# Products into an unread bank in the pauses of TensorE around the scan and in the feed stage

## The chip, the cores and the metric

The kernel runs on one core of one Trainium2 chip (trn2). The metric is the device time of the launch in microseconds (us), lower is better; the figure of a kernel is the median of its runs. One profiled execution gives the trace. In it the clock granted to TensorE is shown as a share of 2.4 GHz: 1.00 is the upper of its two levels, 0.50 is 1.2 GHz.

## What is computed

A decoder of two layers in float32 over x of shape (4, 256, 128), with 16 heads of 8 features. Each of the six blocks reads a layer norm of x and adds its result to x:

```
x = x + L0_attn(layernorm(x))               # cumulative linear attention
x = x + L0_xattn(layernorm(x), ctx)         # cross attention, masked by length
x = x + L0_ffn(layernorm(x))                # two rounds of top-2 of 8 experts
x = x + L1_attn(layernorm(x))               # state space scan, 16 states
x = x + L1_xattn(layernorm(x), ctx)         # cross attention with a bias and a padding mask
x = x + L1_ffn(layernorm(x))                # feed stage: two quantised linear layers
```

The three blocks that matter here:

```
# L1_attn: proj = x @ W_xproj; delta = softplus(proj[:64] @ W_dt + b_dt)
# dA = exp(clip(delta*A)); R = exp(cumsum(log dA)); S = cumsum(delta*B*x / R)
# y = sum over 16 states of C * (R*S)  + x*D
# L1_xattn: softmax(q.k/sqrt(8) + bias, padded keys out) @ v, then @ Wo + bo
def bitlinear(x, w, b):                     # L1_ffn: gelu between two of them
    xq = act_quant(rmsnorm(x))              # rounded to 8 bits with a scale for each row
    return einsum('bsd,fd->bsf', xq, weight_quant(w)) + b
```

## The kernel before

The 1024 tokens lie as 8 tiles (j) of 128 rows; much of the work goes by half, 4 tiles or 512 tokens at a time. There is one program for each engine, written out in order by hand; nothing is scheduled by a planner. An engine runs its program strictly in order and waits where the program has a wait on a semaphore (`wait_ge`), so on TensorE (PE) each product starts only when all that stand before it have been issued. PSUM has eight banks of 128 x 512 float32; `bank(i)` is one of them, and every use of each bank is fixed in the code.

The program of TensorE is the function `_(pe)` at L2108. It calls in turn `self_tensor`, `cross_tensor(pe, 0)`, `experts_tensor`, `half_turn(pe, 1, 5)`, `scan_tensor`, `cross_tensor(pe, 1)` and `feed_tensor`. Three places in it matter.

**Entry of the scan.** `half_turn` (L1365) transposes the second half of the normalised rows XN into bank 5 once VectorE (DVE) has normalised them (L1358). ScalarE (ACT) copies that to XNT (L1370). `scan_tensor` then forms the 64 step inputs (`scan_steps_in`, L1471, into bank 0), the rows of B and C (`scan_rows_in`, L1479, bank 4) and delta (`scan_delta_in`, L1487, bank 1). ACT and DVE make the softplus of it (L1498, L1535) and split the B and C rows (L1526 to L1529). After that comes the loop over 16 states: DVE runs for each state a scan with a floor (`carry`, L1705), a product (`accumulate`, L1711) and a second scan (`advance`, L1718). TensorE spreads rows of B and C over the partitions in it (`row`, L287) and sums the outputs (`gather`, L1571). The result is transposed (L1594) and added to X (L1748).

**Entry of the second cross attention.** In `cross_tensor(pe, 1)` stand in order: `entry_turn` (L266), the transposes of the first normalised half; `first_queries((0, 1))` (L697), the queries of batch 0 for two groups of heads; the first scores (L711, 16 records: 4 heads); `first_queries((2, 3))`; `queries(1)` (L687); then the loop, which begins with scores of two more heads. ACT copies a group of queries to QP (L916) before its scores can run. DVE takes maxima of the scores with the bias added (L988) and, after the first four heads, normalises the second half (L252 to L257), which the next `entry_turn` waits for.

**Feed stage.** The first half of the hidden products runs in the shadow of the cross attention (`feed_turn(pe, 0)`, `feed_first(pe, 0)` to `3`). `feed_tensor` holds the rest: `feed_turn` (L1898) transposes quantised rows of the second half, `feed_first(j)` (L1905) is the first layer for tile j, `turn_hidden(j)` (L1915) transposes the quantised hidden rows of tile j, ACT copies them (L1971), and `second(j)` (L1924) is the second layer. DVE computes the quantisation (L1846, L1849), the hidden rows (L1821), their peaks (L1827), the factors (L1779 to L1790) and adds the result to X (`finish`, L1856). GpSimd (POOL) takes powers for the factors (L1987).

`identb` is the 128 x 128 identity in bfloat16 and `wq1` the quantised weights of the first feed layer, 128 x 512 in bfloat16; both are ready well before the scan.

Of the kernel before, what the change touches and what calls it, by code (L numbers as in the profile page):

```python
# [53 lines left out]
def build(nc, inp, out):  # L54
    ctx = ExitStack()
    with ctx:
        def sb(name, shape, dt=F32):
            return ctx.enter_context(nc.sbuf_tensor(name, shape, dt))
# [3 lines left out]
        def sig(name):  # L62
            if name not in signals:
                signals[name] = ctx.enter_context(nc.semaphore(name))
            return signals[name]
# [21 lines left out]
        identb = sb("identb", [P, P], BF16)  # L87
# [82 lines left out]
        wq1 = sb("wq1", [P, FF], BF16)  # L170
# [12 lines left out]
        def bank(i):  # L183
            return PS[:, i, :]

        def halfbank(i):
            return bank(i).bitcast(BF16)
# [73 lines left out]
        def entry_turn(pe, e, half):  # L261
            pe.wait_ge(sig("xn"), 2 * ENTRY_XN[e] + half + 1)
            if e and half == 1:
                pe.wait_ge(sig("queries"), (e - 1) * B + 2)
            for t in range(4):
                ins = pe.transpose(bank(ENTRY_BANK[e][half])[:, t * P:(t + 1) * P], XN[:, 4 * half + t, :], ident[:, :])  # L266
            ins.then_inc(sig("turned"), 1)
# [6 lines left out]
        def key_bias(dve):  # L274

            dve.wait_ge(sig("const_late"), 1)
            dve.wait_ge(sig("bqk_in"), 16 * HG)
            dve.wait_ge(sig("row_bias"), 1)
            for w, scale in ((0, DH ** -0.5), (1, 1.0)):
                a = rowbias[:, 1, w, :]  # L280
                ins = dve.scalar_tensor_tensor(a, bqk[:, :, w], scale, a, ALU.mult, ALU.add)
            ins.then_inc(sig("bias_rows"), 1)

        def project(pe, first_bank, lhsT, rhs, signal):

            for half in range(2):
                ins = pe.matmul(bank(first_bank + half)[0:lhsT.shape[1], :], lhsT,  # L287
                                rhs[:, half * HALF:(half + 1) * HALF], start=True, stop=True)
            ins.then_inc(sig(signal), 1)
# [377 lines left out]
        def first_query(g):  # L667

            return bank(6 + g % 2)[:, (g // 2) * S:(g // 2 + 1) * S]

        def cross_tensor(pe, L):
# [19 lines left out]
            def first_queries(gs):  # L691

                pe.wait_ge(sig("xnt"), 2 * 5 + 1)
                for g in gs:
                    if g >= 2:
                        pe.wait_ge(sig("query_taken"), g - 1)
                    pe.matmul(first_query(g), WP[:, 1, g, :], XNT[:, 0:S], start=True, stop=True)\  # L697
                        .then_inc(sig("query_part"), 1)
# [98 lines left out]
                ins.then_inc(sig("proj_out"), 1)  # L797

            pe.wait_ge(sig("wp"), 2)
            entry_turn(pe, L + 1, 0)  # L800
            if L == 0:
                queries(0)
            else:
                first_queries((0, 1))
            pe.wait_ge(sig("neg_rows"), 16 * HG * (L + 1))
            pe.wait_ge(sig("key_rows"), 16 * H * (L + 1))
# [301 lines left out]
        def pass_logits(pe, p):  # L1108
            pe.wait_ge(sig("xnt"), 4 + p + 1)
            for t in range(4):  # L1110
                ins = pe.matmul(bank(LOGITS_BANK[p])[:, t * NE:(t + 1) * NE], XNT[:, tokens_of(p)][:, t * P:(t + 1) * P],
                                router[:, :], start=True, stop=True)
            ins.then_inc(sig("logits"), 1)
# [49 lines left out]
        def experts_tensor(pe):  # L1163

            def down(m):

                pe.wait_ge(sig("gated"), 2 * m + 2)
                if m:
                    pe.wait_ge(sig("mixed"), m)
                for t in range(4):  # L1170
                    for c in range(2):
                        ins = pe.matmul(bank(6)[:, t * P:(t + 1) * P], E6[:, (2 * m + c) % 4, t * P:(t + 1) * P],  # L1172
                                        W2[:, m % NE, c, :], start=(c == 0), stop=(c == 1))
                ins.then_inc(sig("down"), 1)

            for g in range(3, UNITS_MOE):
                p, n = divmod(g, UPS)
                unit_up(pe, g)
                if g % 2 == 1:
                    down((g - 3) // 2)  # L1180
                if p + 1 < PASSES and n == 6:
                    pass_turn(pe, p + 1)
                if p + 1 < PASSES and n == 8:
                    pass_logits(pe, p + 1)
                if p == 0 and n in HALVES:
                    context_half_tensor(pe, HALVES.index(n))
                if p == 1 and n in HALVES:
                    keys_half_tensor(pe, HALVES.index(n))
                if p == 1 and n == 14:
                    pe.wait_ge(sig("keys"), 2)  # L1190
                    pe.wait_ge(sig("w_sums"), 1)
                    pe.matmul(bank(7)[:, 0:2], onesf, wscale[:, :], start=True, stop=True).then_inc(sig("w_total"), 1)
                if p == 3 and n == 10:
                    pe.wait_ge(sig("logits_read"), 4)
                    half_turn(pe, 0, 7)
                if p == 3 and n == 12:
                    scan_steps_in(pe, 0, SCAN_BANK[0][0])
                if p == 3 and n == 13:
                    scan_rows_in(pe, 0, SCAN_BANK[0][1])
                if p == 3 and n == 15:  # L1200
                    scan_delta_in(pe, 0, SCAN_BANK[0][2])
            down(UNITS_MOE // 2 - 1)
# [159 lines left out]
        def half_turn(pe, half, bk):  # L1362
            pe.wait_ge(sig("xn"), 2 * 4 + half + 1)
            for t in range(4):
                ins = pe.transpose(bank(bk)[:, t * P:(t + 1) * P], XN[:, 4 * half + t, :], ident[:, :])  # L1365
            ins.then_inc(sig("turned"), 1)
# [527 lines left out]
        def feed_turn(pe, half):  # L1894
            pe.wait_ge(sig("q1"), half + 1)
            for t in range(4):
                j = 4 * half + t
                ins = pe.transpose(halfbank(0)[:, t * P:(t + 1) * P], QB[:, j * P:(j + 1) * P], identb[:, :])  # L1898
            ins.then_inc(sig("q_turned"), 1)

        def feed_first(pe, j):
            pe.wait_ge(sig("qt1"), j // 4 + 1)
            if j >= 2:
                pe.wait_ge(sig("h1_read"), j - 1)
            pe.matmul(bank(1 + j % 2), QTB[:, j * P:(j + 1) * P], wq1[:, :], start=True, stop=True)\  # L1905
                .then_inc(sig("h1"), 1)

        def feed_tensor(pe):

            def turn_hidden(j):  # L1910
                pe.wait_ge(sig("q2"), j + 1)
                if j >= 2:
                    pe.wait_ge(sig("gt"), j - 1)
                for c in range(FF // P):
                    ins = pe.transpose(halfbank(3 + j % 2)[:, c * P:(c + 1) * P], GQ[:, j % 2, c * P:(c + 1) * P],  # L1915
                                       identb[:, :])
                ins.then_inc(sig("g_turned"), 1)

            def second(j):
                pe.wait_ge(sig("gt"), j + 1)  # L1920
                if j >= 2:
                    pe.wait_ge(sig("x_tile"), j - 1)
                for c in range(FF // P):
                    ins = pe.matmul(bank(6 + j % 2)[:, 0:D], GQT[:, j % 2, c * P:(c + 1) * P], wq2[:, c, :],  # L1924
                                    start=(c == 0), stop=(c == FF // P - 1))
                ins.then_inc(sig("h2"), 1)

            feed_turn(pe, 1)
            feed_first(pe, 4)
            feed_first(pe, 5)  # L1930
            turn_hidden(0)
            feed_first(pe, 6)
            second(0)
            turn_hidden(1)
            feed_first(pe, 7)
            second(1)
            turn_hidden(2)
            second(2)
            turn_hidden(3)
            second(3)  # L1940
            turn_hidden(4)
            for j in range(5, NT):
                turn_hidden(j)
                second(j - 1)
            second(NT - 1)

        def feed_root(act, ch):
# [160 lines left out]
        @block.tensor  # L2108
        def _(pe):
            pe.wait_ge(sig("ident"), 1)  # L2110
            entry_turn(pe, 0, 0)
            entry_turn(pe, 0, 1)
            self_tensor(pe)
            cross_tensor(pe, 0)
            experts_tensor(pe)
            half_turn(pe, 1, 5)
            scan_tensor(pe)
            cross_tensor(pe, 1)
            feed_tensor(pe)
# [101 lines left out]
```

## Time and profile before

| | us |
|---|---|
| runs shown | 612.29, 613.69, 617.9 |
| median | 613.69 |
| profiled execution, its device time | 612.31 |
| profiled execution, span from first to last instruction | 610.5 |
| mean granted clock of TensorE in it | 0.913 |

Busy in the span: TensorE 503.1 us (82%), its weight loads 288.7 us, VectorE 451.9 us (74%), ScalarE 263.1 us, GpSimd 134.5 us. The profile has a row for each engine over 40 equal slices of 15.3 us, and one with the granted clock. The chain that ended last follows the end of the program back through whatever released each step. A product in float32 shows in the trace as two records, and each record is preceded by a load of its weights.

### The profile page before, as it was taken

How to read it: one execution, taken by the hardware profiler on the slowest of the kernel's cores; microseconds unless marked ns; L12 is line 12 of the kernel's file. 1: busy time of each engine (PE TensorE's matmuls, PEld its weight loads, DVE VectorE, ACT ScalarE, POOL GpSimd, SP SyncE). 2: the span in 40 equal slices, each digit the busy share in tenths (PEclk: the TensorE clock that was granted, in tenths of full speed). 3: DMA queues.
4: the chain of work that ended last, by engine and by line, in shares of the span. 5: the costliest groups of instructions: out<-in, count | busy, mean ns of one | idle time of the engine just before them, and what ended most of it. 6: DMA issues, size and time to landing. Idle time of an engine off the chain costs nothing.

```text
span 610.5 us, 8920 instructions
## 1 busy us (share of the span) xinstructions
PE 503.1 (82%) x3146; PEld 288.7 (47%) x3146; DVE 451.9 (74%) x1175; ACT 263.1 (43%) x455; POOL 134.5 (22%) x101
## 2 busy tenths in 40 slices
PE   3997799999999999999999545475475999999433
PEld 1344666665666666666665301122123655555212
DVE  6499767776673567666475779999995688888785
ACT  5531356555543244244242345555511444445552
POOL 8443000000000000310000028999980100000100
PEclk9999899999999999999999755978886999999855
DMA  5000160000100000100000000000001000000001
GB/s 131 24 15 1 34 209 2 1 2 2 43 2 0 1 1 5 31 6 0 1 1 1 1 0 0 0 0 1 0 1 43 2 1 2 2 2 1 2 4 30
DMA packets 10767, 9.25 MB, mean 15 GB/s; under 512 B 2050, under 2 KB 9540, under 8 KB 10724
## 3 DMA queue, kind: packets, MB, share of 16 engines
q1 hardware_dynamic: 10724, 8.69, 5.2%
q8 instruction: 25, 0.41, 0.3%
q14 instruction: 18, 0.15, 0.1%
HBM read 6.98 MB, written 0.52 MB: 12 GB/s over the span
## 4 chain that ended last, share of the span: by engine, by line
PE 63%; DVE 29%; ACT 3%; issue 3%; POOL 0%; DVEq 0%; POOLq 0%; ACTq 0%
PE PS L1146 18%; PE PS L711 10%; PE PS L1172 9%; DVE PS L1705 6%; DVE VA L1718 6%; PE PS L774 5%; DVE PS L1711 3%; PE PS L759 3%; PE PS L750 3%; PE PS L687 2%; PE PS L731 2%; PE PS L450 1%; PE PS L428 1%; PE PS L784 1%; DVE E L557 1%
## 5 line engine op out<-in xcount | busy, mean ns | idle before, releaser
L1146 PE MATMUL PS<-XNT,KSA 128*128 128x512 f32 x256 | 118.3, 596 | 0.0
L933 ACT ACTIVATE E<-PS 128x512 f32<-128x512 f32 x128 | 71.2, 596 | 67.2 <-PE PS L759 41.7
L1160 DVE TENSOR_TENSOR E<-E,PS 128x512 f32<-128x512 f32 x64 | 43.9, 687 | 55.3 <-ACT E L1154 54.4
L1154 ACT ACTIVATE E<-PS 128x512 f32<-128x512 f32 x64 | 38.1, 597 | 105.3 <-PE PS L1146 105.0
L759 PE MATMUL PS<-QM,KP 32*128 32x256 f32 x512 | 81.3, 399 | 0.8 <-ACT E L933 0.8
L711 PE MATMUL PS<-KP,QP 32*128 32x256 f32 x512 | 78.2, 409 | 0.8 <-ACT QP L900 0.8
L1172 PEld LDWEIGHTS PS<-KSA,E 128*128 128x128 f32 x512 | 62.1, 192 | 16.0 <-issue 14.7
L1146 PEld LDWEIGHTS PS<-XNT,KSA 128*128 128x128 f32 x256 | 45.2, 191 | 41.5 <-issue 41.3
L1172 PE MATMUL PS<-KSA,E 128*128 128x128 f32 x512 | 62.4, 275 | 0.4 <-DVE XN L1381 0.4
L711 PEld LDWEIGHTS PS<-KP,QP 32*128 32x128 f32 x512 | 51.1, 188 | 20.9 <-issue 10.3
L988 DVE CUSTOM_DVE_ANT_0 SCR<-PS,KSA 128x256 f32<-128x256 f32 x128 | 46.5, 420 | 19.5 <-PE PS L711 18.4
L287 PE MATMUL PS<-KSA,select 128*128 128x512 bf16 x64 | 25.8, 495 | 41.7 <-ACT KSA L1606 31.9
L759 PEld LDWEIGHTS PS<-QM,KP 32*128 32x128 f32 x512 | 53.6, 184 | 3.7 <-issue 3.3
L983 DVE TENSOR_REDUCE MXT<-PS 128x2 f32<-128x512 f32 x64 | 41.1, 686 | 18.1 <-PE PS L711 18.0
L2094 POOL TENSOR_SCALAR KSA<-SCR 128x512 f32<-128x512 f32 x1 | 0.6, 618 | 199.5 <-DVE wq L1775 199.5
L1381 DVE SCALAR_TENSOR_TENSOR XN<-PS,gates,XN 128x128 f32<-128x128 f32 x124 | 34.8, 344 | 7.8 <-PE PS L1172 7.8
L1652 POOL TENSOR_SCALAR OT<-OT 128x1020 f32<-128x1020 f32 x16 | 16.6, 1036 | 101.3 <-ACT OT L1625 100.2
L1571 PE MATMUL PS<-E,ident 128*128 128x512 f32 x60 | 35.6, 726 | 3.2 <-POOL E L1667 3.2
L1705 DVE TENSOR_TENSOR_SCAN PS<-OT,PS 128x1024 f32<-128x1024 f32 x16 | 36.7, 2294 | 0.5
L287 PEld LDWEIGHTS PS<-KSA,select 128*128 128x128 bf16 x64 | 5.2, 108 | 66.3 <-ACT KSA L1606 42.1
L1667 POOL TENSOR_TENSOR E<-VA 128x1024 f32<-128x1024 f32 x15 | 35.2, 2349 | 3.8 <-PE PS L1571 2.9
L1659 POOL TENSOR_TENSOR KSA<-SCR,KSA 128x1024 f32<-128x1024 f32 x15 | 35.2, 2349 | 0.9 <-ACT KSA L1606 0.9
(278 smaller groups left out, 827.8 us busy)
## 6 DMA issues: line engine op xcount, KB each, us to landing
KSA<-in_w SPq DMA_DIRECT2D x2, 1024.0 KB, 6.8
X<-in_x SPq DMA_DIRECT2D x2, 256.0 KB, 3.2
SCR<-in_ctxT SPq DMA_DIRECT2D x1, 512.0 KB, 5.4
KP<-OT SPq DMA_DIRECT2D x16, 32.0 KB
SCR<-in_fside SPq DMA_DIRECT2D x1, 512.0 KB, 4.8
KP<-QM SPq DMA_DIRECT2D x16, 32.0 KB
out_x<-X SPq DMA_DIRECT2D x8, 64.0 KB, 1.5
wx<-in_w_x SPq DMA_DIRECT2D x1, 384.0 KB, 6.5
```

Source lines behind the costliest of these rows:

```text
L711: ins = pe.matmul(score_bank(n, i)[:, q * S:(q + 1) * S], QP[rows(i), g, t:t + P], KP[rows(i), g, b * S:(b + 1) * S], start=True, stop=Tru ...
L759: ins = pe.matmul(o[:, kt * S:(kt + 1) * S], KP[rows(i), g, t:t + P], QM[rows(i), g, b * S:(b + 1) * S], start=not parts_of_bias(j), stop= ...
L933: act.activation(slot(m, j), weight_bank(m, j), ACT.Exp).then_inc(sig("exps"), 1)
L983: ins = dve.tensor_reduce(MXT[:, n % 2, :, c], o, AX, ALU.max, negate=True)
L988: ins = dve.tensor_tensor_reduce(out=BIASED[:, i % 2, q, :], in0=o[:, q, :], in1=BIASQ[:, q, :], scale=-1.0, scalar=3e38, op0=ALU.add, op1 ...
L1146: ins = pe.matmul(bank(2 * (g % 3) + o), w[:, e, c * P:(c + 1) * P], XNT[:, tokens_of(p)], start=True, stop=True)
L1154: act.activation(E6[:, 4 + g % 2, :], bank(2 * (g % 3)), ACT.Silu).then_inc(sig("silu"), 1)
L1160: dve.tensor_tensor(E6[:, g % 4, :], E6[:, 4 + g % 2, :], bank(2 * (g % 3) + 1), ALU.mult)\
L1172: ins = pe.matmul(bank(6)[:, t * P:(t + 1) * P], E6[:, (2 * m + c) % 4, t * P:(t + 1) * P], W2[:, m % NE, c, :], start=(c == 0), stop=(c = ...
L1571: ins = pe.matmul(bank(6 + half), ident[:, :], HC[n % 2][:, half * HALF:(half + 1) * HALF], start=(n == 0), stop=False, skip_group_check=True)
L1705: dve.tensor_tensor_scan(CARRY, DA[n % 3], FLOOR, 0.0, ALU.mult, ALU.add).then_inc(sig("carried"), 1)
L1718: dve.tensor_tensor_scan(HH[n % 2], DA[n % 3], CARRY, 0.0, ALU.mult, ALU.add).then_inc(sig("state"), 1)
```

## The change

A new helper `turn_over(pe, bk, n)` issues n products of `identb` with `wq1` (128x128 by 128x512, bfloat16) into a bank bk. No instruction reads what they write, they carry no semaphore, and they wait for none. 124 of them are put into TensorE's program: 20 ahead of the transposes at the entry of the scan and 2 behind (bank 1), 16 and 2 around the transposes at the entry of the second cross attention (bank 2), and 84 in 16 places of the feed stage (bank 5). Nothing is removed, and the programs of the other engines are the same.

```diff
--- before.py
+++ after.py
@@ -281,6 +281,11 @@
                 ins = dve.scalar_tensor_tensor(a, bqk[:, :, w], scale, a, ALU.mult, ALU.add)
             ins.then_inc(sig("bias_rows"), 1)
 
+        def turn_over(pe, bk, n):
+
+            for _ in range(n):
+                pe.matmul(bank(bk), identb[:, :], wq1[:, :], start=True, stop=True)
+
         def project(pe, first_bank, lhsT, rhs, signal):
 
             for half in range(2):
@@ -797,10 +802,13 @@
                 ins.then_inc(sig("proj_out"), 1)
 
             pe.wait_ge(sig("wp"), 2)
+            if L == 1:
+                turn_over(pe, 2, 16)
             entry_turn(pe, L + 1, 0)
             if L == 0:
                 queries(0)
             else:
+                turn_over(pe, 2, 2)
                 first_queries((0, 1))
             pe.wait_ge(sig("neg_rows"), 16 * HG * (L + 1))
             pe.wait_ge(sig("key_rows"), 16 * H * (L + 1))
@@ -1925,23 +1933,36 @@
                                     start=(c == 0), stop=(c == FF // P - 1))
                 ins.then_inc(sig("h2"), 1)
 
+            turn_over(pe, 5, 28)
             feed_turn(pe, 1)
+            turn_over(pe, 5, 2)
             feed_first(pe, 4)
             feed_first(pe, 5)
+            turn_over(pe, 5, 16)
             turn_hidden(0)
             feed_first(pe, 6)
+            turn_over(pe, 5, 1)
             second(0)
+            turn_over(pe, 5, 2)
             turn_hidden(1)
             feed_first(pe, 7)
+            turn_over(pe, 5, 1)
             second(1)
+            turn_over(pe, 5, 2)
             turn_hidden(2)
+            turn_over(pe, 5, 2)
             second(2)
+            turn_over(pe, 5, 2)
             turn_hidden(3)
+            turn_over(pe, 5, 2)
             second(3)
+            turn_over(pe, 5, 12)
             turn_hidden(4)
             for j in range(5, NT):
+                turn_over(pe, 5, 2)
                 turn_hidden(j)
                 second(j - 1)
+                turn_over(pe, 5, 2)
             second(NT - 1)
 
         def feed_root(act, ch):
@@ -2113,7 +2134,9 @@
             self_tensor(pe)
             cross_tensor(pe, 0)
             experts_tensor(pe)
+            turn_over(pe, 1, 20)
             half_turn(pe, 1, 5)
+            turn_over(pe, 1, 2)
             scan_tensor(pe)
             cross_tensor(pe, 1)
             feed_tensor(pe)
```

TensorE's program at the entry of the scan, before: the last product of the experts (L1172, into which the transposes L1365 follow), up to the spread rows L287.

```order
L1172 MATMUL PS<-KSA,E 128x128 x8
L1365 MATMUL PS<-ident,XN 128x128 x4
L1471 MATMUL PS<-XNT,wssm 64x512
L1479 MATMUL PS<-XNT,wssm 32x512 x4
L1487 MATMUL PS<-SCR,wdt 128x512
L287 MATMUL PS<-KSA,select 128x512 x18
```

The same place in the changed kernel, where lines are numbered 5 to 8 higher and L287 is the new helper (the name `wq` stands for `wq1`).

```order
L1180 MATMUL PS<-KSA,E 128x128 x8
L287 MATMUL PS<-wq,identb 128x512 x20
L1373 MATMUL PS<-ident,XN 128x128 x4
L287 MATMUL PS<-wq,identb 128x512 x2
L1479 MATMUL PS<-XNT,wssm 64x512
L1487 MATMUL PS<-XNT,wssm 32x512 x4
L1495 MATMUL PS<-SCR,wdt 128x512
```

Only the two new rows have come in; the order of the rest is as it was. At the entry of the second cross attention TensorE's program reads, in the changed kernel:

```order
L1602 MATMUL PS<-ident,SCR 128x128 x8
L287 MATMUL PS<-wq,identb 128x512 x16
L266 MATMUL PS<-ident,XN 128x128 x4
L287 MATMUL PS<-wq,identb 128x512 x2
L702 MATMUL PS<-XNT,WP 128x256 x2
L716 MATMUL PS<-KP,QP 128x256 x8
L702 MATMUL PS<-XNT,WP 128x256 x2
L692 MATMUL PS<-XNT,WP 128x256 x4
```

Here too the two rows of L287 are all that is new: one behind the transposes of the scan's result, one behind the transposes of the normalised half. In the feed stage, from the last `feed_first` in the cross attention's shadow on, the changed kernel has:

```order
L1913 MATMUL PS<-wq,SCR 128x512
L287 MATMUL PS<-wq,identb 128x512 x28
L1906 MATMUL PS<-identb,SCR 128x128 x4
L287 MATMUL PS<-wq,identb 128x512 x2
L1913 MATMUL PS<-wq,SCR 128x512 x2
L287 MATMUL PS<-wq,identb 128x512 x16
L1923 MATMUL PS<-identb,SCR 128x128 x4
L1913 MATMUL PS<-wq,SCR 128x512
L287 MATMUL PS<-wq,identb 128x512
L1932 MATMUL PS<-wq,SCR 128x128 x4
L287 MATMUL PS<-wq,identb 128x512 x2
```

L1906, L1913, L1923 and L1932 are the L1898, L1905, L1915 and L1924 of before. Every wait of TensorE in this stage now has one or more products of the helper ahead of it.

## Rows read from the trace of the kernel before

**Rows 1.** Page: granted clock, in tenths, in 40 slices of 15.3 us.

```profile
PEclk9999899999999999999999755978886999999855
```

**Rows 2.** Windows: us, busy us of PE, PEld, DVE, ACT, POOL (records), granted clock, DMA.

```profile
343.50:346.30 2.80, 0.00 (x0) 0.00 (x0) 2.04 (x11) 0.41 (x2) 0.00 (x0) 0.50 0.00 0
380.00:455.00 75.00, 45.56 (x104) 16.69 (x103) 73.69 (x40) 36.23 (x46) 69.56 (x36) 0.86 0.00 0
465.40:473.20 7.80, 7.05 (x29) 4.71 (x30) 1.87 (x11) 2.32 (x6) 0.00 (x0) 0.50 0.14 46
```

**Rows 3.** Timeline of PE at the scan's entry: start, us, line, form [idle before].

```profile
346.34 1.12 PE L1365 MATMUL PS<-ident,XN 128*128 128x128 f32 x4 [5.30 <-DVE XN L1358]
348.24 1.94 PE L1471 MATMUL PS<-XNT,wssm 128*64 128x512 f32 x2 [0.78 <-ACT XNT L1370]
350.11 1.94 PE L1479 MATMUL PS<-XNT,wssm 128*32 128x512 f32 x8
351.97 2.07 PE L1487 MATMUL PS<-SCR,wdt 64*128 64x512 f32 x2
```

**Rows 4.** Timeline of PE: the same kinds at the full clock.

```profile
326.41 1.07 PE L1471 MATMUL PS<-XNT,wssm 128*64 128x512 f32 x2
...
331.11 1.06 PE L1479 MATMUL PS<-XNT,wssm 128*32 128x512 f32 x8
...
337.52 1.12 PE L1487 MATMUL PS<-SCR,wdt 64*128 64x512 f32 x2
...
477.51 0.66 PE L266 MATMUL PS<-ident,XN 128*128 128x128 f32 x4
```

**Rows 5.** Chain that ended last: start us, us, what; three products like the helper's.

```profile
480.85 0.65 PE PS L750 x3
```

**Rows 6.** Timeline of PE, second cross attention's entry; last row of the first's.

```profile
465.39 1.09 PE L266 MATMUL PS<-ident,XN 128*128 128x128 f32 x4 [5.49 <-DVE XN L257]
467.22 2.08 PE L697 MATMUL PS<-XNT,WP 128*128 128x256 f32 x4 [0.74 <-ACT XNT L271]
469.22 2.11 PE L711 MATMUL PS<-KP,QP 32*128 32x256 f32 x16
471.27 2.08 PE L697 MATMUL PS<-XNT,WP 128*128 128x256 f32 x4
473.13 1.94 PE L687 MATMUL PS<-XNT,WP 128*128 128x256 f32 x8
...
68.75 1.17 PE L711 MATMUL PS<-KP,QP 32*128 32x256 f32 x16 [0.77 <-ACT QP L900]
```

**Rows 7.** Timeline of PE in the scan: pauses, and the products behind them.

```profile
407.41 0.60 PE L287 MATMUL PS<-KSA,select 128*128 128x512 bf16 x2 [2.67 <-ACT KSA L1606]
407.85 3.10 PE L1571 MATMUL PS<-E,ident 128*128 128x512 f32 x4
...
425.16 0.61 PE L287 MATMUL PS<-KSA,select 128*128 128x512 bf16 x2 [1.80 <-ACT KSA L1606]
425.60 1.88 PE L1571 MATMUL PS<-E,ident 128*128 128x512 f32 x4
...
454.04 1.99 PE L1571 MATMUL PS<-E,ident 128*128 128x512 f32 x4 [2.62 <-POOL E L1667]
```

**Rows 8.** Timeline of PE in the feed stage; the first row at the full clock.

```profile
567.29 0.39 PE L1898 MATMUL PS<-identb,SCR 128*128 128x128 bf16 x4
...
582.14 0.61 PE L1898 MATMUL PS<-identb,SCR 128*128 128x128 bf16 x4 [7.29 <-DVE SCR L1816]
...
597.09 0.61 PE L1924 MATMUL PS<-wq,SCR 128*128 128x128 bf16 x4 [0.69 <-ACT SCR L1971]
600.74 0.61 PE L1915 MATMUL PS<-identb,SCR 128*128 128x128 bf16 x4 [3.04 <-DVE SCR L1849]
603.94 0.61 PE L1915 MATMUL PS<-identb,SCR 128*128 128x128 bf16 x4 [1.30 <-DVE SCR L1849]
```

**Rows 9.** Timeline of POOL: the power that the second factors wait for.

```profile
596.75 1.01 POOL L1987 TENSOR_TENSOR rs<-ve,exponent 128x4 f32<-128x4 f32 x1 [10.79 <-DVE ve L1835]
```

## The prediction

> **What bounds the kernel now.** I read the page's row of the granted clock first: TensorE runs at its upper level for most of the span and falls from it in the slices around the scan and in the last two and a half [rows 1]. The rest asks, for each of those stretches, whether a slow TensorE is on the path that sets the end. I read that from the chain of waits, then from the timeline of PE.
>
> In the loop of the scan it is not. From 380 to 455 us VectorE is busy 73.69 of 75 us while the clock is only 0.86 on average [rows 2]; the chain goes round in VectorE's three instructions and passes TensorE nowhere. A faster TensorE buys nothing there, and the change puts nothing there.
>
> It is on the path at three places, each behind a pause:
> - Entry of the scan. PE pauses 5.30 us for the last normalised half [rows 3]. The clock is at 0.50 from 343.5 us on [rows 2], so the transposes, step inputs, B and C rows and delta all run at 1.2 GHz, end to end, and ACT and DVE wait behind them.
> - Entry of the second cross attention. PE pauses 5.49 us [rows 6]; from 465.4 to 473.2 us it is busy 7.05 of 7.8 us at 0.50 [rows 2].
> - Feed stage. The first pause is 7.29 us [rows 8], and the clock stays low to the end [rows 1]. DVE sets most of this stage; TensorE is only in some links of it.
>
> **Entry of the scan, term A.** The change fills the pause with 20 products. The nearest row is L750, the same shape (128x128 identity, 512 columns, bfloat16): three take 0.65 us on the chain at full clock, 0.217 each [rows 5]. 20 take 4.33 us of the 5.30, so 0.97 us is left idle and the transposes aren't held up. The two products behind them (0.43 us) lie in the 0.78 us in which PE waits for ACT's copy [rows 3]. If the clock stays up, each row at the slow clock is exchanged for the same kind at the full one [rows 3, 4]: transposes 1.12 to 0.66 (0.46), step inputs 1.94 to 1.07 (0.87), B and C rows 1.94 to 1.06 (0.88), delta 2.07 to 1.12 (0.95). A = 3.2 us. They lie on the chain one behind the other. What is late next is DVE's and ACT's own work on delta, which moves along with them. After it PE goes idle and the clock may fall again; the spread rows (L287) are then slow as before, and the loop doesn't care.
>
> **Entry of the second cross attention, term B.** 16 products take 3.47 us of 5.49, which leaves a pause of 2.02 us; then transposes, and two products (0.43 us) in a gap of 0.74 us [rows 6]. At full clock: transposes 1.09 to 0.66 (0.43) [rows 4, 6]; first scores 2.11 to 1.17, by the same 16 records of the first cross attention (0.94) [rows 6]; each pair of queries (L697) has no row at full clock, so I scale L687, the same shape, eight in 1.94 us of which half is 0.97 to 1.1 with its tail: 2.08 to 1.08, twice (2.0) [rows 6]. Sum 3.37. ACT's copy of the first queries would then be ready just behind the second pair of them, not ahead, which I put at 0.1 us. B = 3.3 us. DVE starts its maxima earlier by the same amount, and its normalisation of the second half, which the next transposes wait for, still ends before PE arrives there, so the gain isn't given back. The bias that DVE adds later is loaded long before.
>
> Does the clock stay up through a pause of 2.02 us? The scan shows both outcomes. Behind a pause of 1.80 us four products took 1.88 us, all at full clock; behind one of 2.62 us they took 1.99; but behind one of 2.67 us they took 3.10, so the clock was lost in between [rows 7]. A pause of 2.02 lies among these, and what follows it is thin: transposes, 0.43 us of products and a small gap. I hold B for a little more likely kept than lost. In A (0.97 us left) and in the feed stage below I hold it for likely.
>
> **Feed stage, term C.** 28 products take 6.08 us of the 7.29, 12 take 2.6 of the 3.04, and the four between later tiles 0.87 of 1.30 [rows 8]; the groups of one and two lie under ACT's copies (0.69 us idle before L1924 [rows 8]). Four bfloat16 transposes take 0.61 us slow and 0.39 fast [rows 8], so each such group on the chain is worth 0.22. Where transposes and second layer run back to back at the end of a round, both count, 0.44. On the chain: the transposes at 582.14 (0.22); nothing from then to 595 us, where the chain runs through ACT and DVE and leaves PE out; nothing in the round of tile 3 either, though the chain shows PE there: the products end at 597.70, but POOL's power for the next factors ends at 597.76 [rows 8, 9], so it takes PE's place; then the rounds of tiles 5, 6 and 7 (0.44 each). C = 1.5 us.
>
> **Cost.** No engine but PE gets an instruction, no queue is passed and no wait is added, so what a product can hold up is only what stands behind it in PE's order. At full clock all of it fits, cost 0. At the slow clock one takes about 0.43 (twice 0.217), and the fit is gone: see the second and last rival.
>
> **Sum.** Against the profiled execution's own 612.31 us: 612.31 - 3.2 - 3.3 - 1.5 = 604.3. The median of the runs stands 1.4 us above that execution. I take this as scatter that the change leaves alone: where the clock happens to be low at the end of the scan, a set of output sums there takes 3.10 instead of 1.88 us [rows 7], and those are on the chain. So 605.7 against the median of 613.69.
>
> **A rule beside it.** At full clock four float32 transposes take 0.66 us and at the slow clock 1.09 [rows 4, 6]; so they follow the clock, and A and B count them. The Trainium skill ("TensorE: Matmul & The Clock Gate", Part 4, PE-mode transpose) says that the full clock does not engage for transposes, which don't count as busy in the same way. On the duration the trace disagrees (by that half of the rule A, B and C would shrink by 0.46, 0.43 and four times 0.22, and the time be 607.5; it gets no chance). On the other half no row here decides. If they don't count, the stretch behind the remaining 2.02 us pause looks emptier still; that is my second case below with a mechanism, at 609.1, and I leave its chance as that case has it.
>
> **The rivals.**
> 1. All three kept: 605.7. Chance 0.45.
> 2. The clock falls in the 2.02 us pause all the same. B is lost, and the two products behind the transposes run slow, 0.87 us in a 0.74 us gap, 0.1 late: 612.31 - 4.7 + 0.1 = 607.7, with the 1.4 us 609.1. For it: the 2.67 us pause. Against: 2.62 us survived. In part (the clock back sooner than before) it ends between. Chance 0.32.
> 3. The feed stage falls too, since every tile's round holds short pauses: C gone, A and B kept, 612.31 - 6.5 = 605.8, or 607.2. Chance 0.1.
> 4. The products don't hold the clock anywhere but cost nothing: within 1 us of 613.7. Against: L750, the same product among others, runs at the full clock [rows 5]. Chance 0.08.
> 5. Slower. The products run at 1.2 GHz: 20 take 8.7 us against 5.30 (3.4 late), 28 take 12.2 against 7.29 (4.9 late), 12 take 5.2 against 3.04 (2.2 late), the four 1.7 against 1.30 (0.4, three times), 16 take 6.9 against 5.49 (1.5): 13 us, 627. It decides only if the clock falls before the products start. A filler run may have 0.97 / 0.217, about 4, slow ones of 20 before it delays anything. The run follows on dense work at full clock in all three places, so I give 0.05.
>
> **How the numbers follow.** The forecast is that of case 1, 605.7. The range goes down to no scatter and a B fuller by the 0.1 and by more in executions that stayed slow for longer: 603.3; and up past case 2 with its scatter: 610.0. About 1%, 6.1 us, is what a measurement of this kernel can tell from no change: the border is 607.55. Case 1 gives 0.38 below it, case 3 0.07, case 2 0.08: faster 0.53. Slower by over 1% only in case 5: 0.04. The rest, 0.43, within 1%.
>
> **What would show it.** In the profile after: the granted clock at 1.00 from the last expert product to delta, with L1471, L1479 and L1487 (now L1479, L1487, L1495) near 1.07 us each; the scan's first step 3.2 us earlier from the last expert product; the loop still 5.9 us for each state. For B, the clock row between the last transposes of the scan and the first scores, and those at 1.17 us. For C, groups of four transposes at 0.39 us to the end, and the round of tile 3 no shorter. I am wrong if the clock is up and a place isn't shorter (then something else stood right behind TensorE, most likely in C, where POOL and DVE are close), or if rows of the helper are what L1373, L266 or L1923 wait for.

## The result

The changed kernel takes 609.35 us, the median of 15 runs (607.46 to 611.78); the kernel before takes 613.69 us over 15 runs beside them (611.14 to 618.17). The ratio is 0.9937, with a 95% interval of 0.9914 to 0.9960: about 4 us less, half of the 8.0 us forecast. The time lies within the forecast range, but the size of the gain was wrong, and its main term, B, is where it failed.

A count given ahead of the prediction is too high: the diff adds up to 122 products and not 124, with 82 in 17 places of the feed stage and not 84 in 16. The traces agree: the trace of the changed kernel has 122 loads of the products' weights, that of the kernel with the feed stage's products alone has 82. No price in the prediction hangs on it.

The profiled execution took 611.73 us, span 610.0, mean granted clock 0.944 (0.913 before). Its row of the granted clock, in 40 slices, answers to [rows 1]:

```profile
PEclk9999799999998899999999985987788999999899
```

The low slices at the end are gone, and those around the scan are fewer. But there are new low tenths in the middle, where the program is as before: in the experts the clock fell twice, for 3.4 us each. The timeline of PE there (start, us, line, form) shows what one such fall costs:

```profile
184.86 1.88 PE L1154 MATMUL PS<-XNT,KSA 128*128 128x512 f32 x4
...
189.91 3.53 PE L1154 MATMUL PS<-XNT,KSA 128*128 128x512 f32 x4
```

The same four records take 1.88 us at full clock and 3.53 behind the fall, 1.65 more. With a third fall at 152 us and a longer one at 63 us, the last expert product ends at 346.81 us here and at 341.05 in the profile of before. So the two profiled executions differ by only 0.5 us in their spans, though the three places that the change touches are 6.3 us shorter. At the entry of the scan, the timeline of PE, to be read against [rows 3]:

```profile
344.79 2.02 PE L1180 MATMUL PS<-KSA,E 128*128 128x128 f32 x16 [0.38 <-DVE XN L1389]
346.87 4.26 PE L287 MATMUL PS<-wq,identb 128*128 128x512 bf16 x19
352.12 0.66 PE L1373 MATMUL PS<-ident,XN 128*128 128x128 f32 x4 [0.99 <-DVE XN L1366]
352.62 0.59 PE L287 MATMUL PS<-wq,identb 128*128 128x512 bf16 x2
353.56 1.04 PE L1479 MATMUL PS<-XNT,wssm 128*64 128x512 f32 x2 [0.35 <-ACT XNT L1378]
354.53 1.06 PE L1487 MATMUL PS<-XNT,wssm 128*32 128x512 f32 x8
355.53 1.12 PE L1495 MATMUL PS<-SCR,wdt 64*128 64x512 f32 x2
```

(One record of the 20 is missing from the trace.) 0.99 us of the pause is left, 0.97 was forecast; each of the four groups has the full clock's duration, and the loop starts 17.27 us after the last expert product instead of 20.42. At the entry of the second cross attention, to be read against [rows 6]:

```profile
462.56 3.40 PE L287 MATMUL PS<-wq,identb 128*128 128x512 bf16 x15
467.90 0.66 PE L266 MATMUL PS<-ident,XN 128*128 128x128 f32 x4 [1.94 <-DVE XN L257]
468.40 0.59 PE L287 MATMUL PS<-wq,identb 128*128 128x512 bf16 x2
469.31 1.88 PE L702 MATMUL PS<-XNT,WP 128*128 128x256 f32 x4 [0.32 <-ACT XNT L271]
471.12 2.04 PE L716 MATMUL PS<-KP,QP 32*128 32x256 f32 x16
473.08 1.13 PE L702 MATMUL PS<-XNT,WP 128*128 128x256 f32 x4
```

Behind the 1.94 us that are left of the pause the clock is lost all the same, but later than the forecast's second case has it. The transposes and the two products behind them are still fast (granted clock 1.00 from 467.90 to 469.30 us); then most of the first queries and the first scores are slow (0.50 from 469.60 to 472.90 us), and the second queries are fast again. In the feed stage, to be read against [rows 8]:

```profile
575.33 0.60 PE L1913 MATMUL PS<-wq,SCR 128*128 128x512 bf16 x1
575.72 7.72 PE L287 MATMUL PS<-wq,identb 128*128 128x512 bf16 x28
583.28 0.39 PE L1906 MATMUL PS<-identb,SCR 128*128 128x128 bf16 x4
...
606.16 0.40 PE L1923 MATMUL PS<-identb,SCR 128*128 128x128 bf16 x4 [0.44 <-DVE SCR L1857]
606.39 0.39 PE L1932 MATMUL PS<-wq,SCR 128*128 128x128 bf16 x4
```

The clock had fallen at 575.4 us, so the 28 products took 7.72 us instead of the 6.1 counted, and no idle time stands before L1906: the transposes were held up by 0.3 us. To the end of the program every group of four then takes 0.39 or 0.40 us.

### The profile page after: what moved, and what is told of

Its sections match the earlier page's. It is cut to its first block, busy times and chain, and to the rows that moved or that the text cites. A ratio compares the mean times of both kernels' runs of the same rounds, so it can differ in the third digit from the quotient of the medians.

```text
span 610.0 us, 9155 instructions
## 1 busy us (share of the span) xinstructions
PE 526.7 (86%) x3260; PEld 298.6 (49%) x3268; DVE 452.4 (74%) x1175; ACT 263.2 (43%) x455; POOL 134.5 (22%) x101
## 4 chain that ended last, share of the span: by engine, by line
PE 66%; DVE 23%; issue 5%; ACT 4%; POOL 2%; POOLq 0%; DVEq 0%; ACTq 0%
PE PS L1154 18%; PE PS L716 10%; PE PS L1180 9%; PE PS L779 5%; DVE PS L1713 5%; DVE VA L1726 5%; PE PS L764 3%; PE PS L755 3%; DVE PS L1719 2%; PE PS L692 2%; PE PS L736 2%; PE PS L455 1%; PE PS L287 1%; PE PS L433 1%; PE PS L789 1%
## 5 line engine op out<-in xcount | busy, mean ns | idle before, releaser
L1154 PE MATMUL PS<-XNT,KSA 128*128 128x512 f32 x256 | 121.5, 609 | 0.0
L779 PE MATMUL PS<-E,VX 128*32 128x256 f32 x512 | 35.2, 393 | 0.7 <-ACT E L941 0.7
```

Of the source, the lines that this page charges most:

```text
L779: ins = pe.matmul(bank(6)[rows(i), (g % 2) * S:(g % 2) * S + S], VX[:, QT * b + kt, HG * g + i, :], slot(m, j)[:, kt * S:(kt + 1) * S], st ...
L1154: ins = pe.matmul(bank(2 * (g % 3) + o), w[:, e, c * P:(c + 1) * P], XNT[:, tokens_of(p)], start=True, stop=True)
```

## Experiments

The theories, as the expectations number them. **Theory 1:** what the change is worth at its three places can be read in each trace, B is worth less than forecast because the clock falls in the 2 us left of its pause, and what else moves comes from falls of the clock elsewhere, the same in both kernels. **Theory 2:** the new products delay the dense part ahead of them. **Theory 3:** a clock kept at one place falls at the next, so the gain is given back. **Theory 4:** the falls in the experts come from one-row products there. A fall is a stretch in which the granted clock is at the lower level.

All are edits of the changed kernel unless said otherwise. Since one trace shows one execution, I read each trace by stretches: to the last expert product; from there to the first scan instruction of DVE; from there to the end of the transposed result (the loop); from there to the first L750 product (the entry of the second cross attention); and the feed stage from the transposes in the cross attention's shadow to the end. (Where an expectation gives the entry of the second cross attention as 20.95 and 19.2 us, it is the stretch that has 20.79 and 19.03 us here.) The cross attention between the last two takes 86.60 to 86.62 us in all the traces in which both of its ends could be read.

| trace | products | to experts' end | scan entry | loop | cross entry | feed |
|---|---|---|---|---|---|---|
| before | none | 341.05 | 20.42 | 98.43 | 20.79 | 43.25 |
| none | none | 342.70 | 20.43 | 98.43 | 20.76 | 43.24 |
| none2 | none | 341.71 | 19.51 | 98.44 | 20.39 | 43.24 |
| scan_entry | 22 | 340.73 | 17.26 | 98.44 | 20.65 | 43.27 |
| cross_entry | 18 | 342.42 | 19.48 | 99.56 | 17.71 | 43.26 |
| feed | 82 | 342.75 | 20.43 | 98.43 | 20.79 | 41.57 |
| after | 122 | 346.81 | 17.27 | 98.44 | 19.03 | 41.85 |
| again | 122 | 338.50 | 17.26 | 99.67 | 18.94 | 41.85 |
| look1 | 122 | 344.15 | 17.26 | 99.67 | 18.93 | 41.87 |
| look2 | 122 | 341.20 | 17.26 | 98.43 | 20.41 | 41.58 |
| look3 | 122 | 339.15 | 17.27 | 99.60 | 19.03 | 41.84 |
| pause24 | 130 | 341.08 | 17.26 | 98.44 | 17.71 | 41.56 |
| rows128 | none | 335.89 | 19.20 | 99.77 | 19.58 | 43.44 |
| all | 127 and 4 others | 336.90 | 17.26 | 99.26 | 17.71 | 41.57 |

**None of the products**, as a control: every call of the helper replaced by `pass`.

> None of the 124 products, the rest of the changed kernel as it is: the kernel before in other words. Every theory: ratio 1.000 within its interval. What it is for is its trace, a second execution of the kernel before. Theory 1 (the clock also falls at random in the dense parts ahead of the scan, the same in both kernels): the last expert product ends somewhere between 341 and 347 us, not at one place, and the granted clock shows short stretches at 0.50 ahead of 340 us wherever it ends late. Theory 2 (the products delay the dense part of the changed kernel): it ends at 341 us as in the profile of the kernel before, with no stretch at 0.50 between 70 and 340 us.

614.05 us against 613.04 of before, ratio 1.0034 (1.0011 to 1.0057). (The ratio is not simply that of the two medians, which is 1.0016.) The two have the same instructions, and still the interval leaves out 1. So a ratio here can be off by another 0.3%, about 2 us, beyond its interval, and verdicts on single terms of 1 or 2 us have to come from the stretches of the traces. The trace fits theory 1: its experts end at 342.70 us, with one fall of the clock in them.

**Only the scan's entry:** the two calls at the second cross attention and all 13 of the feed stage are replaced.

```diff
-                turn_over(pe, 2, 16)
+                pass
...
-                turn_over(pe, 2, 2)
+                pass
...
-            turn_over(pe, 5, 28)
+            pass
...
```

> Only the 22 products at the entry of the scan. From the end of the last expert product to the first scan instruction of DVE: 17.3 us against 20.4, as in the changed kernel. Theory 1: ratio 0.9950 (3.1 us off), all of it kept to the end. Theory 3 (a gain at one place is lost at the next pause, since the clock falls there all the same): less than half of it is left at the end, ratio above 0.997.

610.06 us, ratio 0.9944 (0.9923 to 0.9965), the largest of the three single parts, with 17.26 us at the scan's entry and the stretches behind it as before. The ratio is that of 3.4 us, and the trace shows none of the 3.2 us lost at the next pause (20.65 us there, 20.79 before); theory 3 falls.

**Only the second cross attention's entry:** the calls of the feed stage and these are replaced.

```diff
-            turn_over(pe, 1, 20)
+            pass
             half_turn(pe, 1, 5)
-            turn_over(pe, 1, 2)
+            pass
```

> Only the 18 products at the entry of the second cross attention. From the end of the transposes of the scan's result to the first group of L750: 20.95 us before, 19.2 in the profile of the changed kernel, where the clock fell for 3.4 us. Theory 1 (a pause of 2 us is left, in which the clock falls in most executions): 19 to 20.9 us, ratio 0.997. Forecast's theory (the clock is kept): 17.6 us, ratio 0.9946.

612.58 us, ratio 0.9988 (0.9959 to 1.0016). In its trace the clock held, and the entry took 17.71 us, 3.1 less: the rows of PE show what B is worth when it is kept.

```profile
466.84 0.65 PE L266 MATMUL PS<-ident,XN 128*128 128x128 f32 x4 [1.94 <-DVE XN L257]
467.34 0.59 PE L287 MATMUL PS<-wq,identb 128*128 128x512 bf16 x2
468.25 1.13 PE L702 MATMUL PS<-XNT,WP 128*128 128x256 f32 x4 [0.32 <-ACT XNT L271]
469.60 1.17 PE L716 MATMUL PS<-KP,QP 32*128 32x256 f32 x16 [0.23 <-ACT QP L924]
```

The runs together show less: 0.5 us by the medians against the kernel before, and 1.5 against the kernel without the products, which ran beside them. In how many of them the clock held can't be read from the times. The 1.94 us of pause that are left are the same here as in the changed kernel, so that pause can be survived.

**Only the feed stage:** the calls at both entries are replaced.

```diff
-            turn_over(pe, 1, 20)
+            pass
...
-                turn_over(pe, 2, 16)
+                pass
...
```

> Only the 84 products of the feed stage. Forecast's theory: 1.5 us, ratio 0.9975. Rival: the first run of 28 holds up the transposes behind it (by 0.3 us in the profile of the changed kernel, where it took 7.7 us instead of 6.1 because the clock was at 0.50 for 3.4 us), so 1.2 us or less, ratio 0.998 or above.

611.85 us, ratio 0.9992 (0.9971 to 1.0013), which by itself tells nothing from no change. Its trace has 41.57 us against 43.25 in the feed stage, 1.7 less, with no fall of the clock there.

**The changed kernel again**, and three more single executions of it:

> The changed kernel a second time, for a second trace of it and to see by how much a repeated comparison moves. Theory 1 (what the change is worth at its three places is fixed within 1.5 us; the rest of the difference between two executions comes from falls of the clock ahead of the scan): from the last expert product to the scan loop 17.3 us again; entry of the second cross attention 17.7 (clock kept) or 19 to 21 us (fallen); feed stage 41.5 to 41.9; the experts 185.8 us or 1.65 us more for each fall of the clock in them. Ratio 0.990 to 0.994. Theory 2 (the products delay the dense part): the first cross attention and the experts together again 288 us against 282.4.

607.99 us, ratio 0.9911 (0.9875 to 0.9946). In this trace the experts take 185.84 us, as before, and the first cross attention 97.4 us against 96.6: together 283 us, not the 288 of theory 2. So the products do not slow the dense part ahead of them; theory 2 falls. The cross entry took 18.94 us.

> The changed kernel once more, for its trace alone. What is open is how often the clock survives the 2 us that are left of the pause at the entry of the second cross attention: it fell in both traces so far (19.0 and 18.9 us) and held in the one with the products only there (17.7). Theory 1: 17.7 when it holds, 18.9 to 21 when it falls, nothing between; more falls than holds. The forecast's chance (held in 4 or 5 of 10) would want 17.7 in one or two of three looks. Scan entry 17.3 and cross attention 86.6 in each.

> As the look before: 17.7 us or 18.9 to 21 us at the entry of the second cross attention, 17.3 at the scan's entry, 41.5 to 41.9 in the feed stage; the experts 185.8 us plus 1.65 for each fall of the clock in them.

> As the two looks before. If all three traces show 17.7 us, the size of B was right and what was missing of the gain lies in the scatter alone; if none does, B is worth about 1.8 us with 16 products.

One execution each: 610.19, 607.21 and 605.21 us. The cross entry took 18.93, 20.41 and 19.03 us. With the two earlier traces that makes none kept in five; with the trace of `cross_entry`, which has the same products at this place, one in six. In look2 the fall lasted longer, and even the projections behind the scores are slow:

```profile
462.28 0.66 PE L266 MATMUL PS<-ident,XN 128*128 128x128 f32 x4 [1.94 <-DVE XN L257]
462.78 0.68 PE L287 MATMUL PS<-wq,identb 128*128 128x512 bf16 x2
463.69 2.08 PE L702 MATMUL PS<-XNT,WP 128*128 128x256 f32 x4 [0.23 <-ACT XNT L271]
465.69 2.11 PE L716 MATMUL PS<-KP,QP 32*128 32x256 f32 x16
467.73 2.08 PE L702 MATMUL PS<-XNT,WP 128*128 128x256 f32 x4
469.60 2.08 PE L692 MATMUL PS<-XNT,WP 128*128 128x256 f32 x8
```

The scan's entry is 17.26 or 17.27 us in all of them, as expected. In look2 the clock was up at the start of the feed stage as well, and the run of 28 took what was counted for it, with the transposes waiting for DVE and not for the run:

```profile
571.29 6.21 PE L287 MATMUL PS<-wq,identb 128*128 128x512 bf16 x28
578.76 0.40 PE L1906 MATMUL PS<-identb,SCR 128*128 128x128 bf16 x4 [1.26 <-DVE SCR L1824]
```

look3 shows the loop's weak place, the last sums of the outputs, here behind a fall of the clock; the same four records take 1.99 us in the row of before at 454.04 us [rows 7]:

```profile
449.12 3.68 PE L1579 MATMUL PS<-E,ident 128*128 128x512 f32 x4 [2.63 <-POOL E L1675]
```

**The kernel without the products again:**

> The kernel without the products once more, for a third trace of it: 20.4 us at the scan's entry, 20.8 at the second cross attention's, 43.2 in the feed stage. Theory 1: these three do not move, so that the gain per place does not depend on the execution of before; the rest of its span (self attention, first cross attention, experts, end of the scan) moves by 1 to 6 us.

One execution, 611.66 us. The scan's entry took 19.51 us and not 20.4: the clock fell as before but came back sooner, so that delta, the last of the four groups, was fast (1.16 us; the other three slow, 1.11, 1.94 and 1.93):

```profile
347.01 1.11 PE L1373 MATMUL PS<-ident,XN 128*128 128x128 f32 x4 [5.30 <-DVE XN L1366]
348.90 1.94 PE L1479 MATMUL PS<-XNT,wssm 128*64 128x512 f32 x2 [0.78 <-ACT XNT L1378]
350.77 1.93 PE L1487 MATMUL PS<-XNT,wssm 128*32 128x512 f32 x8
352.64 1.16 PE L1495 MATMUL PS<-SCR,wdt 64*128 64x512 f32 x2
```

So my expectation was wrong that the stretches of before are the same in every execution; what the products save is 3.15 us in one and 2.25 in another.

**24 products instead of 16** at the second cross attention's entry:

```diff
-                turn_over(pe, 2, 16)
+                turn_over(pe, 2, 24)
```

> The changed kernel with 24 products instead of 16 ahead of the transposes at the entry of the second cross attention: 5.2 us of the pause of 5.5, so about 0.3 us of it is left instead of 2. Theory 1 (what loses B is the clock falling in the 2 us that are left): entry 17.7 us with no stretch at 0.50 in it, ratio below that of the changed kernel by 0.002. Rival (other things set that entry): 19 us or more all the same. If the clock is low when the run begins, the products are slow and the transposes come late by up to 1.5 us.

605.28 us, ratio 0.9874 (0.9848 to 0.9899), beside 0.9911 for the changed kernel in the same comparison: 2.7 us less by the medians, though the intervals overlap. Its trace:

```profile
462.17 0.66 PE L266 MATMUL PS<-ident,XN 128*128 128x128 f32 x4 [0.22 <-DVE XN L257]
462.66 0.59 PE L287 MATMUL PS<-wq,identb 128*128 128x512 bf16 x2
463.57 1.13 PE L702 MATMUL PS<-XNT,WP 128*128 128x256 f32 x4 [0.31 <-ACT XNT L271]
464.93 1.17 PE L716 MATMUL PS<-KP,QP 32*128 32x256 f32 x16 [0.22 <-ACT QP L924]
```

0.22 us of the pause is left instead of 1.94, every group is fast, and the entry takes 17.71 us. The rival, that something else sets that entry, falls: it has the 17.71 us of `cross_entry`, where the clock held. That the fuller pause is what holds the clock rests on few traces (held in two of two with 24 products, this one and `all`, and in one of six with 16) and on the ratio, which points the same way.

**Full rows for the bias products** of the experts stage, on the kernel without the helper's products:

```diff
-        brow = sb("brow", [1, D])
+        brow = sb("brow", [P, D])
...
-                ins = pe.matmul(o, onesf[0:1, :], brow[0:1, :], start=False, stop=True)
+                ins = pe.matmul(o, onesf, brow[:, :], start=False, stop=True)
...
+            pool.memset(brow[:, :], 0.0)
```

> The kernel before, but the products that add the value bias of the second cross attention in the experts (eight float32 products, one row deep: a row of ones with the bias row) are made 128 rows deep, of a full matrix of ones and a bias tile that is zero below its first row: the same sum, in the same number and size of records. Theory 4 (the falls of the clock near 186 to 200 us come from these thin products): no fall between 180 and 205 us, experts 185.8 us. Rival (the falls there are at random or belong to the whole stretch of short products): falls in 2 of 3 executions as before, 187.5 or 189.2 us in this profile. Ratio 0.998 by theory 4, 1.000 by the rival.

609.41 us, ratio 0.9931 (0.9899 to 0.9962). There is no fall in that stretch, as theory 4 says, and none in the trace of the last kernel below, which has this edit too. But falls in the experts stood in only 4 of the 12 traces of kernels with the thin products, so two traces without any decide nothing. What it shows beyond doubt I had not expected: the experts take 182.76 us, 3.1 less than the 185.84 of an execution without falls. The timeline of PE, first before, then here:

```profile
184.43 0.48 PE L1126 MATMUL PS<-brow,masks 1*128 1x128 f32 x2
184.84 0.49 PE L1125 MATMUL PS<-wx,SCR 128*128 128x128 f32 x2
185.26 0.48 PE L1126 MATMUL PS<-brow,masks 1*128 1x128 f32 x2
```

```profile
182.26 0.39 PE L1134 MATMUL PS<-brow,masks 128*128 128x128 f32 x2
182.48 0.39 PE L1133 MATMUL PS<-wx,SCR 128*128 128x128 f32 x2
182.71 0.39 PE L1134 MATMUL PS<-brow,masks 128*128 128x128 f32 x2
```

From one bias product to the next it is 0.83 us before and 0.45 here, and there are eight. Two more things in the table bear on the sums below: without any product of the helper the scan's entry took 19.20 us here and the second cross attention's 19.58, because the clock came back sooner by itself.

**All together:** the changed kernel with 24 products at the cross entry, 25 instead of 28 at the start of the feed stage, the full-row bias products, and a filled pause at the entry of the first cross attention:

```diff
             pe.wait_ge(sig("wp"), 2)
+            if L == 0:
+                pe.wait_ge(sig("weighed_sum"), NT - 1)
+                for _ in range(4):
+                    pe.matmul(bank(0), ident[:, :], wfeat[:, :, :].rearrange("p w d -> p (w d)"), start=True, stop=True)
```

> All together: the changed kernel with 24 products at the entry of the second cross attention, 25 instead of 28 at the start of the feed stage, the 128-row bias products, and four new float32 products (identity with the 128x512 weights of the first attention, into bank 0, 0.86 us each at full clock) in the 4.2 us pause at the entry of the first cross attention. Theory 1: self attention's end to the first expert product 95 us against 96.6 to 99.1, experts 185.8, scan entry 17.3, second cross entry 17.7, feed stage 41.4: some 8 to 10 us below the kernel before, ratio 0.985 to 0.987. Rival (each kept pause only moves the fall to the next one): 0.992 or above.

601.40 us (598.04 to 602.23), ratio 0.9803 (0.9773 to 0.9833): it beats both kernels, by more than I expected. From the end of the self attention to the first expert product it takes 95.31 us (96.54 to 99.06 in all others), experts 182.75, scan entry 17.26, cross entry 17.71. In the trace the clock falls only in the scan, where nothing waits for TensorE but at the loop's end:

```profile
PEclk9999999999999999999999975888779999999999
```

The four new products and the 25 were not run by themselves; that the stretch with the four is shorter than in any of the 13 other traces is all that speaks for them.

## Why the prediction was wrong, step by step

**What bounds the kernel:** right. The loop never got faster by a better clock: 98.43 us in both kernels. It has a weak place at its end, which I had named only as scatter: where the clock falls in the last output sums it takes 99.3 to 99.8 us.

**Term A:** the mechanism and the durations were right (3.15 us against 3.2, with 0.99 us of the pause left). As a term for the median it was somewhat too large, because I took the cost of the slow clock from one execution of before. Over the three traces without the products or any other edit the entry takes 20.12 us on average, so A is 2.9. (Over all six traces with no product at this place, `cross_entry`, `feed` and `rows128` among them, it takes 19.91 us, and A is 2.6.)

**Term B is the step that failed.** I held B for a little more likely kept than lost, from pauses in the scan of 1.80 and 2.62 us that the clock survived. Its size when kept was right: 3.1 us against 3.3. But in five traces of the changed kernel it was never kept, and the entry takes 19.27 us on average against 20.65, so B is 1.4 (1.2 against the 20.49 us of all six traces with no product at this place). Case 2 of the rivals had the mechanism, but not what is left of B: the clock falls only behind the transposes, and in four of the five traces it is back for the second queries, so part of the 3.3 us stays. That its 609.1 us lies 0.25 us from the median is partly luck: it gives up all of B, and leaves out what A and the loop's end lacked. The scan's pauses were the wrong measure: they bracket 2.02 us, but did not tell what this one would do. There, runs of float32 products stand near the pause on either side; here it is followed by four transposes, two short products and another gap. That this is the reason is not shown, and it can't be all of it, since `cross_entry` kept the clock in the same surroundings. That the clock held in both traces with the pause filled to 0.22 us (pause24 and "all") says that the rest of the pause had a part in it; what decides at 1.94 us stays open. Of how much the transposes count (the rule of the Trainium skill, "TensorE: Matmul & The Clock Gate", Part 4, weighed in the prediction) no run here decides anything; their duration follows the clock at all three places.

**Term C:** right in size, 1.4 us (41.80 on average against 43.24) for 1.5 forecast, and the round of tile 3 did not become shorter, as POOL's power sets it: its two powers start 11.81 us apart in both profiles, before and after. One reason given was wrong: that the run of 28 follows dense work at full clock. The clock falls just ahead of it in four of the five traces of the changed kernel, and the run then holds up the transposes by 0.3 us (41.85 instead of 41.57). This is the last rival, at a small part of its price.

**The 1.4 us on top for scatter** was of the right kind, but the scatter is larger and sits elsewhere than I said: the time up to the last expert product runs from 338.5 to 346.8 us in kernels with the same code up to there. Part of that are the falls at the first cross attention's entry and in the experts. As much comes from the start of the program: the self attention ends between 55.3 and 59.8 us, since TensorE comes to the full clock's durations at different times, which the row of the granted clock doesn't show. The same product, first in the trace of look1, then of again:

```profile
14.91 2.08 PE L433 MATMUL PS<-wfeat,XNT 128*128 128x512 f32 x2
```

```profile
14.99 1.13 PE L433 MATMUL PS<-wfeat,XNT 128*128 128x512 f32 x2
```

**The sum, corrected:** 2.9 + 1.4 + 1.4 = 5.7 us at the three places. In the five traces the loop is 0.7 us longer on average and the part ahead of the scan 0.1 us (341.96 against 341.82), which leaves 4.9 us. The comparisons say 3.9 us (0.9937) and 5.5 us (0.9911). Of the 8.0 us forecast, B lacks 1.9, the loop's end 0.7, A 0.3 and C 0.1; the last 1 us between 4.9 and 3.9 is within what a comparison can be off by. Whether the products have a part in the falls at the loop's end (three of five traces with all of them, none of three without any) is open: it happened in six of the fourteen traces, in kernels with and without products.

## What to carry to other kernels

When TensorE waits in front of a part that it sets itself, a run of products that nobody reads can buy back the slow clock: at the scan's entry it gave 3.15 us of the 3.16 that the rows at the two levels differ by. Try a pause filled nearly to its end before one with 2 us left, count what the run costs if it starts at the slow clock (0.3 us at the start of the feed stage here), and don't judge what is left by pauses from other surroundings. Take the cost of a slow clock from several executions and by stretches of the program: the ratio of the feed stage's products alone (0.9992) told nothing, while their stretch was 1.7 us shorter, beside a scatter of 8 us elsewhere. And look at what TensorE multiplies in its dense parts too: 3 us lay in eight products of depth one.

## What the runs showed of the hardware

- The granted clock can fall in a stretch without idle time. In the profile after it fell at 189.6 and 199.9 us, and PE was busy in all of the 3.3 us before each, with 128-column products of which every second one is a single row deep. Each fall cost 1.65 us. Whether the one-row products are the reason is open: such falls stand in 4 of 12 traces with them and in none of 2 without.
- Float32 products of one row, alternating with products of 128 rows, made the pair dearer and not cheaper: 0.83 us for the two, against 0.45 when both use all 128 rows.
- With the same 1.94 us of pause left ahead of the same instructions, the clock fell in five traces and held in one. It did not fall in the pause itself but behind it: in the profile after, 1.00 until 469.3 us, 1.4 us into the work that follows.
- Two builds with the same instructions had a ratio of 1.0034 over 12 and 33 runs, with an interval (1.0011 to 1.0057) that leaves out 1.
